# A typed graph layer: all edge rows gathered from the finished message table, none from x ahead of it

## What is computed

```
h   = relu(layernorm(x))                       # per node
msg = h[src] @ W[type] + b[type]               # per edge, 128 -> 128
out = x + segment_sum(msg, dst)                # per node
```

## Time and profile before

| | us |
|---|---|
| median of 3 executions | 2442.58 (2439.0 to 2455.74) |
| the profiled execution | 2435.22 |
| its span, first to last instruction | 2433.3 |
| table stage, to the last bias addition | 260 |
| first gather of table rows issued | 278.5 |
| last (partial) superblock's first gather issued | 2409.3 |

### The profile page before, as it was taken

One profiled execution on the slowest core, in us unless ns is written; L12 is line 12 of the kernel. 1 busy time (PEld: TensorE's weight loads), 2 busy tenths in 40 slices (PEclk: granted clock), 3 DMA queues, 4 the chain that ended last, 5 costly groups with the idle time before them and its releaser, 6 DMA issues. The chain is left out here.

```text
span 2433.3 us, 19156 instructions
## 1 busy us (share of the span) xinstructions
PE 859.1 (35%) x4100; PEld 668.3 (27%) x4101; DVE 629.8 (26%) x1552; ACT 135.1 (6%) x384; POOL 1481.2 (61%) x1574
## 2 busy tenths in 40 slices
PE   3249322423233243323332324242415142322354
PEld 1014222222222233222322223222314132222244
DVE  2029611313131222222222222222213131211143
ACT  1016100000000000000000000000000000000000
POOL 7740367566666666566666666757666666566643
PEclk7559656667576666667666666666667576665577
DMA  6237311111111111111111111111111111511122
GB/s 176 79 99 275 106 46 49 37 45 46 44 48 44 43 45 46 38 46 45 46 45 46 45 46 43 49 38 49 42 46 44 45 46 47 143 49 45 45 84 80
DMA packets 107774, 151.12 MB, mean 62 GB/s; under 512 B 27235, under 2 KB 69937, under 8 KB 107745
## 3 DMA queue, kind: packets, MB, share of 16 engines
q0 software_dynamic: 50016, 102.53, 16.1%
q1 hardware_dynamic: 53335, 45.89, 5.9%
q10 hardware_dynamic: 4394, 2.40, 0.4%
HBM read 118.62 MB, written 32.09 MB: 62 GB/s over the span
## 5 line engine op out<-in xcount | busy, mean ns | idle before, releaser
L389 POOL DMA_INDIRECT messages<-message_table,table_row x1155 | 1093.2, 946 | 629.7 <-issue 343.7
L829 PE MATMUL ps_sum<-lists,messages 128*128 128x128 f32 x1632 | 280.9, 347 | 745.5 <-DVE acc L626 493.6
L829 PEld LDWEIGHTS ps_sum<-lists,messages 128*128 128x128 f32 x1632 | 266.2, 257 | 757.6 <-issue 757.3
L389 POOL DMA_INDIRECT lists<-message_table,table_row x288 | 272.4, 946 | 259.9 <-PEq L810 181.7
L829 PE MATMUL ps_sum<-lists 128*128 128x128 f32 x608 | 115.2, 367 | 374.4 <-issue 340.4
L663 DVE SCALAR_TENSOR_TENSOR stage<-ps_i,lists,key_col 128x1024 f32<-128x1024 f32 x60 | 76.4, 1282 | 563.6 <-PE ps_y L857 278.8
L829 PEld LDWEIGHTS ps_sum<-lists 128*128 128x128 f32 x608 | 109.7, 279 | 378.5 <-issue 378.5
L634 DVE SCALAR_TENSOR_TENSOR lists<-ps_node,lists,dst_col 128x512 f32<-128x512 f32 x272 | 193.0, 747 | 63.8 <-issue 43.5
L626 DVE TENSOR_TENSOR acc<-acc,ps_sum x209 | 58.9, 282 | 550.6 <-remote 496.1
L770 PE MATMUL ps_y<-w_sb,h_t 128*128 128x512 f32 x196 | 123.1, 724 | 97.5 <-issue 97.1
L857 PE MATMUL ps_y<-stage 128*128 128x512 f32 x240 | 124.4, 663 | 59.0 <-DVE stage L663 47.7
(11 more groups left out here) (90 smaller groups left out, 539.3 us busy)
## 6 DMA issues: line engine op xcount, KB each, us to landing
message_table<-stage SPq DMA_DIRECT2D x98, 256.0 KB
messages<-message_table,table_row POOLq DMA_INDIRECT x1155
early_x<-in_x SPq DMA_DIRECT2D x6, 896.0 KB
out<-acc SPq DMA_DIRECT2D x6, 896.0 KB
lists<-message_table,table_row POOLq DMA_INDIRECT x288
acc<-in_x SPq DMA_DIRECT2D x4, 896.0 KB
early_x<-in_x,src_col POOLq DMA_INDIRECT x120
acc<-in_x ACTq DMA_DIRECT2D x2, 896.0 KB, 5.8
```

Of the source, the lines that this page charges most:

```text
L389: pool.indirect_dma_start(messages[k][:, t, :], None, table_rows, bass.IndirectOffsetOnAxis(ap=flat_rows[:, at + t:at + t + 1], axis=0)).t ...
L829: ins = nc.tensor.matmul(ps_sum[:, bass.ds(q % BANKS, 1), 0:d], still, moves, start=(t == 0), stop=(t == tiles - 1))
```

## The change

The early rows are gone, with all that worked on them: the 120 gathers of x, the statistics, the key one-hot, their matmuls and copies, their constants and buffers, and the extra loads (`b_rows`, a separate load of the first chunk of `src`). All 195 full superblocks gather from the table: 39 rounds of five (`rounds = full_sbs // SLOTS`, `spare` is 0), of which 37 are in the plain loop and 2 with aligned tiles. The transposed sums get a buffer of their own, `sums`, which GpSimd zeroes at the start; `acc` keeps x, so the memset of `acc` (L560) goes and x is not loaded again (L336 to L341). `WINDOW` is a constant of 128, so shapes stay as they were.

```diff
-    rounds = (full_sbs - EARLY_SBS) // SLOTS
+    rounds = full_sbs // SLOTS
+    spare = full_sbs - rounds * SLOTS
+    sums = sb("sums", [P, node_tiles * P + WINDOW])
...
-            sp.wait_ge(e_used, EARLY_SBS + 1)
-            for at in range(0, node_tiles, GROUP):
-                tiles = min(GROUP, full_node_tiles - at)
-                sp.dma_start(x_rows[:, at:at + tiles, :], ...).then_inc(x_reloaded, 16)
...
-            pool.wait_ge(early_cols, 1)
-            for t in range(early_tiles):
-                pool.indirect_dma_start(early_x[:, t, :], None, x,
-                                        bass.IndirectOffsetOnAxis(ap=src_col[:, t:t + 1], axis=0)).then_inc(early_gathered, 16)
+            pool.memset(sums[:, :], 0.0).then_inc(sums_cleared, 1)
...
             groups_of(dve, dve_group)
-            dve.wait_ge(h_ready, node_tiles)
-            nc.vector.memset(acc[:, :, :], 0.0).then_inc(acc_cleared, 1)
...
-            with dve.Fori(0, EARLY_SBS) as i:
-                s = EARLY_SBS + i * (EARLY_ROUNDS * SLOTS)
-                for m in range(EARLY_ROUNDS * SLOTS):
-                    superblock(s + m, onehots[m % SLOTS], m % SLOTS, SB_TILES)
-                    if m == LAG:
-                        early_rows(i)
-                    elif m == 2 * LAG:
-                        early_norm(i)
-                superblock(i, early_onehot, SLOTS, SB_TILES, early=True)
-            with dve.Fori(EARLY_SBS * EARLY_ROUNDS, window_rounds) as i:
+            with dve.Fori(0, window_rounds) as i:
                 for k in range(SLOTS):
-                    superblock(EARLY_SBS + i * SLOTS + k, onehots[k], k, SB_TILES)
+                    superblock(i * SLOTS + k, onehots[k], k, SB_TILES)
...
-            with pe.Fori(0, EARLY_SBS) as i:
-                for m in range(EARLY_ROUNDS):
-                    table_round(i * EARLY_ROUNDS + m, SLOTS - 1 if m else None)
-                early_superblock(i)
-            table_round(EARLY_SBS * EARLY_ROUNDS, None)
-            with pe.Fori(EARLY_SBS * EARLY_ROUNDS + 1, window_rounds) as i:
+            table_round(0, None)
+            with pe.Fori(1, window_rounds) as i:
                 table_round(i, SLOTS - 1)
```

More of the change, by code:

```diff
@@ L32 @@
 SB_TILES = 8
+WINDOW = 128
 SLOTS = 5
@@ L131, in gnn_program @@
     index_f = stage[:, Y_SLOTS * ydim:Y_SLOTS * ydim + 4 * P].rearrange("p (m n) -> p m n", n=P)
[L134 to L142, removed]
     y_flat = stage[:, 0:Y_SLOTS * ydim]
[L146 to L149, removed]
     last_touch = y_flat[0:1, 0:len(STORE_TILES) * (full_sbs + 1)].rearrange("p (n s) -> p n s", s=full_sbs + 1)
[L152 to L157, removed]
+    assert len(STORE_TILES) * (full_sbs + 1) <= Y_SLOTS * ydim
     own_messages = sb("messages", [P, SLOTS - 1, SB_TILES, d])
@@ L295, in load_chunks @@
                              ).then_inc(signal, 16)
-            load_chunks(src_rows, src, 0, 1, loaded_src0)
-            load_chunks(src_rows, src, 1, 2, loaded_first)
-            for rows, dram in lists[1:]:
+            for rows, dram in lists:
                 load_chunks(rows, dram, 0, 2, loaded_first)
@@ L395, in _ @@
                     gather(i, k)
-            gather(rounds, 0, last_tiles)
+            for k in range(spare):
+                gather(rounds, k)
+            gather(rounds, spare, last_tiles)
         @block.scalar
@@ L450, in _ @@
             groups_of(act, act_group)
[L453 to L462, removed]
-                first, windows, regs = load_windows(act, i)
-                with act.Fori(0, windows):
-                    p = pair()
-                    act.wait_ge(key_onehot_free, p * (SB_TILES // 2) + (SB_TILES // 2 + 2))
-                    nc.scalar.copy(h_sums[:, :, :], ps_y[:, 0, :].rearrange("f (t n) -> f t n", n=P))
-                    nc.scalar.copy(edge_counts[:, :], ps_y[:, 1, 0:P]).then_inc(h_sums_ready, 1)
-                    act.reg_add(pair_reg, pair_reg, 1)
-                for r in regs:
-                    act.free_register(r)
         @block.vector
@@ L619, in _, with add_sums @@
             column_regs = [counter(dve, f"column_{n}_before")[0] for n in range(1, LAG + 1)]
-            def add_sums(q, before, ahead=0):
+            def add_sums(q, before, into, columns, ahead=0):
                 column = dve.snap(before, min_val=0, max_val=node_tiles * P - 1)
@@ L624, in add_sums, with make_onehot @@
                 dve.wait_ge(pair_done, q + ahead)
-                at = flat_acc[:, bass.ds(column, P)]
-                return nc.vector.tensor_tensor(at, at, ps_sum[:, bass.ds((q + (1 + ahead)) % BANKS, 1), 0:d], ALU.add)
+                at = into[:, bass.ds(column, columns)]
+                return nc.vector.tensor_tensor(at, at, ps_sum[:, bass.ds((q + (BANKS - LAG + ahead)) % BANKS, 1), 0:columns], ALU.add)
             def pairs_needed():
                 return dve.snap(needed_reg, min_val=1, max_val=max_pairs + LAG)
-            def make_onehot(s, home, tiles, base, needed):
+            def make_onehot(s, home, tiles, base, needed, columns):
                 for half, (a, z) in enumerate(halves(tiles)):
@@ L647, in next_pair, with superblock @@
                 dve.reg_add(pair_reg, pair_reg, 1)
-            def superblock(s, home, base_at, tiles, early=False):
+            def superblock(s, home, base_at, tiles):
                 first, windows, regs = load_windows(dve, s)
@@ L743, in _ @@
                 for k in range(SLOTS):
-                    own_superblock(EARLY_SBS + i * SLOTS + k, onehots[k], SB_TILES)
-            own_superblock(full_sbs, onehots[0], last_tiles)
+                    own_superblock(i * SLOTS + k, onehots[k], SB_TILES)
+            for k in range(spare):
+                own_superblock(rounds * SLOTS + k, onehots[k], SB_TILES)
+            own_superblock(full_sbs, onehots[spare], last_tiles)
             last = pair()
             for n in range(LAG):
-                add_sums(last, column_regs[LAG - 1 - n], n).then_inc(pair_added, 1)
+                add_sums(last, column_regs[LAG - 1 - n], flat_acc, P, n).then_inc(pair_added, 1)
             dve.wait_ge(pair_added, last + LAG)
@@ L895, in _ @@
                 table_round(i, SLOTS - 1, True)
-            superblock(full_sbs, 0, last_tiles, rounds * 16 * SB_TILES + 16 * last_tiles, None, True)
+            for k in range(spare):
+                superblock(rounds * SLOTS + k, k, SB_TILES, (rounds + 1) * (16 * SB_TILES), None, True)
+            superblock(full_sbs, spare, last_tiles, rounds * 16 * SB_TILES + 16 * last_tiles, None, True)
 _INS = ["x", "src", "dst", "edge_type_4", "L0_gnn_W", "L0_gnn_b"]
```

198 lines of the change are left out of this document (40 added, 158 removed).

## The result

In the runs that belong to the prediction the changed kernel takes 2408.19 us (median of 4, 2403.3 to 2408.66) against 2440.79 us before (median of 4, 2434.83 to 2455.74): ratio 0.987, 95% interval 0.983 to 0.991. The forecast was 2414.9 us, ratio 0.989. Later runs add something that this pair does not show. Both kernels have two levels of time, and a set of runs (the kernel before and those run beside it, on one chip) lies wholly on one of them. In three sets the kernel before took 2426 to 2459 us, in three others 1970 to 1972 us. At the lower level the unedited changed kernel was run in one set and was slower, 2095.04 us, ratio 1.063 (1.061 to 1.065).

The account below looks back on a forecast made before the run. Bound: GpSimd's gathers and waits in the edge stage, gathers slowing other engines in the table stage. Terms -138.8, -59.3 and +170.4 give -27.7 us, from 2442.6 to 2414.9 us; range 2374 to 2480 us.

Parts of the forecast that it names:

- The table stage speeds up when the gathers leave it: Table stage: without the 120 early gathers, tiles take 1.139 us instead of 9.1; last bias addition at 132 us, not 260.25.
- the 3 us for a hold-up of stores: Table stage: 3 us added because table stores wait for the initial loads to leave the queue; bounds 0 and 15 us.
- The way from it to the first gather: Between the stages: 7.7 us (3.3 and 4.4) once the memset of `acc` goes; first table gather at 139.7 us.
- GpSimd's memset of the sums is hidden: Kernel start: zeroing `sums` takes 20 us, ends a hundred microseconds before its first reader, and costs nothing.
- A round costs 56.8 us instead of 58.5: Edge stage, plain rounds: without early passes 34 rounds are cheaper by 59.3 us; three more rounds cost 170.4 us.
- The last rounds with the turning stay at 140.3 us: End of the edge stage: the last two rounds, in which sums are turned, keep their 140.3 us.
- the adding in place: Edge stage: x in `acc` is added without a reload; counted as nothing, 0 to 5 us either way for contention.
- Dearer rounds: Edge stage: rounds stay at 58.5 us because long waits belong to the gathers; 64 us more, 2479 us; chance 0.20.
- Table stage as slow as before: Table stage: no speedup without early gathers, only the memset saved; first gather at 267.9 us, 2543 us; chance 0.05.
- The waits vanish: Edge stage: a loop body of one round ends the stalls; rounds of 50.1 us, 2167 us in all; chance 0.05.
- the early passes' 59 us: Edge stage: dropping the 15 passes over early superblocks makes 34 rounds cheaper by 59.3 us.

Follow-up runs that it names:

- the second set: Changed kernel, unedited, on another chip beside the kernel before at 2433.18 us: 2415.13 us, ratio 0.9930, plain rounds 57.00 us.
- the plain loads: Changed kernel plus 120 plain 64 KB loads of x on GpSimd's queue in the table stage: 2111.94, 2109.87 and 2107.3 us.
- the probe: Changed kernel plus 120 indirect gathers of x on GpSimd in the table stage, read by nobody: 2552.27 us in one execution.

## Why the prediction was right, and where it was not

At the level at which its profile was taken the forecast held, 2408.2 us for 2414.9, and the mechanism was the one it named: a stream of gathers that slows the other engines, and ends when it pauses. Two things were luck. The errors of the terms, -8.6, -4.2 and +6.9 us, partly cancel. And the runs that tested it fell on the same level; at the other one the same sum would have had the wrong sign.

- *The table stage speeds up when the gathers leave it.* Right, and shown by putting them back (+137 us). The last bias addition began at 125.81 us, not 132: the 3 us for a hold-up of stores did not come, the first bias addition came 0.7 us earlier, and a tile took 1.115 us, not 1.139. The way from it to the first gather took 5.3 us, not 7.7. Together the term was 8.6 us too long.
- *GpSimd's memset of the sums is hidden.* Right, and with 10.65 us half of the 20 us estimated; it ends at 12.9 us.
- *A round costs 56.8 us instead of 58.5.* Right: 56.69 here, 57.00 in the second set, 56.77 in the kernel before without passes. Of the four cycles that it was read from, the last ends at 2304.39 us, in the aligned rounds, which begin at 2269 us; the number is the same without it. Taking it from the plain loop of before, with the same code, was the best step of the forecast.
- *The last rounds with the turning stay at 140.3 us.* Mis-sized: 147.24 us. The wait of 20.26 us in the earlier trace rows has become one of 27.07 us:

```profile
2300.68 0.94 POOL L329 DMA_INDIRECT lists<-message_table,table_row  x1 [27.07 <-PEq L664]
```

The other traces at this level have 28.50 us there (the changed kernel again, the stretch 148.2 us), 23.32 us (gathers put back, 142.9 us) and 19.42 us (the kernel before without passes, 139.7 us). So all three traces with the changed kernel's end and five slots are longer than the two with the old one, by 2.7 to 8.5 us; with six slots the wait is 20.26 us. At the lower level the same stretch is 99.9 us in both. Whether this is the adding in place, which the forecast put at 0 to 5 us, or the point of its cycle at which the stream meets the turning, was not separated.

- *Dearer rounds.* Fell: 56.69 us, and 57.00 in the repeat, both under the 57.55 us from which the rival decides. *Table stage as slow as before* fell too: 1.115 us a tile.
- *The waits vanish.* The forecast gave it 0.05 and tied it to the loop body. As a mechanism it fell: the body of two rounds had 56.77 us too. At the lower level the waits are gone with the very same code, and then the gain in the table stage shrinks too, since there is little to relieve. The forecast's sum assumed that the slowdown belongs to the kernel. Its one profile could not show otherwise, and neither could the runs beside it; what it should have carried is a case "the disturbance is not there", with rounds of 50 us in *both* kernels. An estimate of that case from its own rows is +131 us on some 1990, a ratio of 1.07: the table's gathers start behind the early ones at 159 us before and at 139.7 after, and three rounds are 150.3 us.

What stays open: what sets the level. It is not the kernel (both kernels have both levels) and not the chip alone (one chip showed both, in different sets at different times). Whether only transfers by a list of rows slow the engines, or any of GpSimd's, was not told apart: the plain loads ran three times, each time at the level without bursts. The late raises of `pair_done` show where the other engines are held. Why a raise is late, and why a superblock then costs 11.36 us, was not shown.

## What to carry to other kernels

When engines with work to do stand still and start again as another engine's stream of DMAs pauses, find out first whether they always do: run the kernel unedited on other chips and at other times, and read a change at each level, since the same edit was worth -1.3% and -0.7% in two sets at one and +6.3% at the other. Moving a stream out of another stage's way pays what it slows there and costs its own length at the end: 139 against 170 us in the forecast's sum with the slowdown, where the early passes' 59 us tip it; 29 against 150 us without it. Before calling an engine slow, compare when its last product ended with when the semaphore behind it was raised. A cost taken from a loop of the old kernel that already has the new one's code and order is better than any sum of single instructions.

## What I had not expected of the hardware

- Two levels of time for one program, 1970.8 and about 2435 us (+24%), with no level between in six sets of runs. In one set at the lower level 7 runs lie within 0.1%, in one at the upper 9 runs within 0.6%.
- At the upper level the raise of a semaphore by TensorE is recorded 8.2 to 23.2 us (medians of six traces) behind the end of the products, beside a stream of gathers; at the lower level 0.01 us.
- At the upper level the pace is strikingly even: four superblocks in 45.4 us with five slots and with six, or three in 34.3 us.
- The slowdown outlasts its cause: the last gather of the probe starts at 162.5 us, and table tiles are slow until 181.07 us.
- GpSimd clears 128 by 12672 elements in 10.65 us, as fast as VectorE did, though its 128 columns had taken 0.20 us.
- At the lower level a memset of 0.12 us behind every gather is free: the gather's period is 1.25 us with it and without it.
